# Matmuls of 96 and 128 output rows cut into column tiles of 32 rows, in a fused two-layer MetaFormer kernel

## The reference, cut to what matters

```python
# layer 0, conv block, MID = 576
h = silu(bn(einsum('nchw,oc->nohw', ln_c(x), w_exp)))          # 96 -> 576
h = silu(bn(depthwise_3x3(h, w_dw)))
s = sigmoid(silu(h.mean((2, 3)) @ w_se1.T + b_se1) @ w_se2.T + b_se2)
x = x + (bn(einsum('nchw,oc->nohw', h * s, w_proj)) + ln_c(x))  # 576 -> 96
# both layers, feed-forward, all operands rounded to fp8e5, sums to fp16
t = t + qlinear(relu(qlinear(ln_t(t), W1, b1)), W2, b2)         # 96 -> 384 -> 96
# layer 1, conv block
g = gelu(group_norm1(conv1x1(ln_c(x), w1, b1)))
g = gelu(w21 on two shifts of g) + gelu(w22 on two shifts of g) # four terms
x = x + conv1x1(group_norm1(g), w3, b3)
```

## Time and profile before

| | |
|---|---|
| median of 3 runs | 6858.68 us (6851.56 to 6858.77) |
| the profiled execution | 6854.27 us, its span 6852.4 us |
| PE busy | 5730.9 us, 84% of the span |
| DVE busy | 5543.4 us, 81% |
| ACT busy | 4409.0 us, 64% |
| mean granted TensorE clock | 0.959 |

### The profile page before, as it was taken

How to read it: one execution, slowest core, us unless ns; L and a number is a source line. 1 busy time by engine, 2 the same in 40 slices (tenths; PEclk the granted TensorE clock), 3 DMA queues, 4 the chain that set the end, 5 groups by cost and what they waited for, 6 DMA issues and landing times.

```text
span 6852.4 us, 111430 instructions
## 1 busy us (share of the span) xinstructions
PE 5730.9 (84%) x40192; PEld 2277.5 (33%) x40192; DVE 5543.4 (81%) x9325; ACT 4409.0 (64%) x7671; POOL 452.6 (7%) x366
## 2 busy tenths in 40 slices
PE   2788888888888888888888888888888888888875
PEld 0333333333333333333333333333333333333332
DVE  4788888888888888888888888888888888888863
ACT  1466766666766666766666766666766666766654
POOL 1000000000000000000000000000000000000000
PEclk9899999999999999999999999999999999999997
DMA  1233323333323333323323323333323323323322
GB/s 41 63 76 86 94 73 86 91 76 85 96 71 85 93 76 85 96 71 87 92 76 85 96 73 86 90 76 84 96 70 85 94 76 84 96 67 88 87 59 62
DMA packets 395481, 556.45 MB, mean 81 GB/s; under 512 B 71490, under 2 KB 391427, under 8 KB 391771
## 3 DMA queue, kind: packets, MB, share of 16 engines
q1 hardware_dynamic: 394940, 549.32, 31.7%
HBM read 233.66 MB, written 78.68 MB: 46 GB/s over the span
## 4 chain that ended last, share of the span: by engine, by line
PE 45%; DVE 31%; ACT 10%; DMA 6%; issue 5%; SPq 4%; DVEq 0%; ACTq 0%; POOL 0%; POOLq 0%
DVE conv L859 16%; PE bank L583 10%; PE bank L598 6%; PE bank L557 4%; PE bank L535 3%; PE bank L585 3%; PE b_banks L682 3%; PE b_banks L639 2%; PE bank L544 2%; DVE hidden L914 2%; PE b_banks L663 2%; ACT hidden L782 2%; PE b_banks L618 2%; DVE xn L906 2%; DVE x L924 2%
## 5 line engine op out<-in xcount | busy, mean ns | idle before, releaser
L859 DVE SCALAR_TENSOR_TENSOR conv<-mid,w_dw,conv 128x1568 f32<-128x1568 f32 x1536 | 2893.7, 1884 | 20.4
L663 PE MATMUL b_banks<-shifted,w_combo 128*32 128x392 f32 x6144 | 681.1, 580 | 311.9 <-DMA shifted<-g 257.8
L535 PE MATMUL bank<-xc_a,w_exp 128*128 128x392 f32 x1536 | 654.9, 525 | 110.1 <-DVE xc_a L842 34.0
L583 PE MATMUL bank<-conv,w_proj_gated 128*96 128x392 f32 x2048 | 728.8, 499 | 4.8 <-DVE x L885 0.5
L598 PE MATMUL bank<-x,centering 128*96 128x392 f32 x1536 | 645.1, 515 | 74.2 <-DVE x L924 39.5
L775 ACT ACTIVATE hidden<-b_banks 128x1176 f16<-128x1176 f32 x512 | 590.0, 1152 | 139.5 <-PE b_banks L618 135.0
L782 ACT ACTIVATE hidden<-hidden 128x1176 fp8e5<-128x1176 f16 x512 | 607.4, 1186 | 39.4 <-DVE hidden L914 39.2
L1001 POOL TENSOR_TENSOR x<-x,xc_a 96x392 f32<-96x392 f32 x256 | 433.2, 1693 | 1729.9 <-DVE xc_a L842 1729.9
L722 ACT ACTIVATE phases<-bank 128x448 f32<-128x448 f32 x384 | 208.5, 543 | 515.5 <-PE bank L544 422.6
L691 ACT ACTIVATE g<-bank 96x392 f32<-96x392 f32 x512 | 256.8, 502 | 337.9 <-PE bank L598 289.6
L618 PE MATMUL b_banks<-xn,w_q 128*128 128x392 fp8e5 x1536 | 348.4, 336 | 133.8 <-ACT hidden L775 116.8
(11 more groups left out here) (157 smaller groups left out, 8112.3 us busy)
## 6 DMA issues: line engine op xcount, KB each, us to landing
phases_on<-phases SPq DMA_DIRECT2D x768, 101.5 KB, 2.6
shifted<-g SPq DMA_DIRECT2D x512, 149.6 KB, 2.7
r_b<-rstd_row_b SPq DMA_DIRECT2D x512, 147.0 KB, 3.0
shifted<-g SPq DMA_DIRECT2D x256, 199.5 KB, 3.0
x<-in_x SPq DMA_DIRECT2D x32, 1176.0 KB, 8.0
r_a<-rstd_row_a SPq DMA_DIRECT2D x256, 147.0 KB, 3.2
x_plus_norm<-x SPq DMA_DIRECT2D x256, 147.0 KB, 2.8
r_a<-x_plus_norm SPq DMA_DIRECT2D x256, 147.0 KB, 2.5
```

Of the source, the lines that this page charges most:

```text
L535: mm(ring[bank][:, 0:TW], WEXP[:, 128 * k:128 * k + 128], xc_tile(t, 128), start=True, stop=True)\
L583: mm(o, WPS[:, k, :], tile(conv(k, t // NTH, parity), t % NTH, 128), start=(k == 0), stop=False)
L663: last = mm(rows(PB[32 * u:32 * u + 32, m, 0:TW]), WC[:, u // 2, 32 * m:32 * m + 32], SH[t % 2][:, u, :].rearrange("p (h w) -> p h w", w=G ...
L859: v.scalar_tensor_tensor(out=acc, in0=src, scalar=WDW[:, k, j:j + 1], in1=acc, op0=ALU.mult, op1=ALU.add).then_inc(sem["convolved"], 1)
```

## The change

A helper `columns` issues every product of 96 or 128 output rows as three or four matmuls of 32 output rows, each at its own output partitions, all with the same moving operand. All f32 full-width products and the fp8 products of `up` and `down` go through it; `se2`, the two `gn` steps and `gn_weights` stay as they were. The last chunk of `proj` now reads all 128 partitions of `ACC4`, with weights that are zero for the half that isn't the tile's; for this `WP` and `WPS` have a sixth chunk, the gate multiplies it in an instruction of its own, and the setup fills it.

```diff
+        def columns(o, weights, x, start=True, stop=True):
+
+            for j in range(0, weights.shape[-1], QUAD):
+                last = mm(o[j:j + QUAD, :], weights[:, j:j + QUAD], x, start=start, stop=stop)
+            return last
...
-                mm(ring[bank][:, 0:TW], WEXP[:, 128 * k:128 * k + 128], xc_tile(t, 128), start=True, stop=True)\
+                columns(ring[bank][:, 0:TW], WEXP[:, 128 * k:128 * k + 128], xc_tile(t, 128))\
                     .then_inc(sem["expanded"], 1)
...
                 for k in range(NCH):
-                    mm(o, WPS[:, k, :], tile(conv(k, t // NTH, parity), t % NTH, 128), start=(k == 0), stop=False)
-                h = t // NTH
-                mm(o, WPS[CW * h:CW * h + CW, NCH, :],
-                   ACC4[CW * h:CW * h + CW, (t % NTH) * TW:(t % NTH + 1) * TW], start=False, stop=True)\
+                    columns(o, WPS[:, k, :], tile(conv(k, t // NTH, parity), t % NTH, 128), start=(k == 0), stop=False)
+                columns(o, WPS[:, NCH + t // NTH, :], tile(ACC4, t % NTH, 128), start=False, stop=True)\
                     .then_inc(sem["projected"], 1)
...
                 for c in range(NHC):
-                    last = mm(PB[:, c, 0:TW], W1Q[:, f, 128 * c:128 * c + 128], XN8[t % 2][:, :],
-                              start=True, stop=True)
+                    last = columns(PB[:, c, 0:TW], W1Q[:, f, 128 * c:128 * c + 128], XN8[t % 2][:, :])
...
-                v.tensor_tensor(WPS[:, :, :], WP[:, :, :],
-                                GATE[:, 2, :].unsqueeze(2).to_broadcast([128, NCK, C]), ALU.mult)\
+                v.tensor_tensor(WPS[:, 0:NCK, :], WP[:, 0:NCK, :],
+                                GATE[:, 2, :].unsqueeze(2).to_broadcast([128, NCK, C]), ALU.mult)
+                v.tensor_scalar(WPS[CW:128, NCK, :], WP[CW:128, NCK, :], GATE[CW:128, 2, NCH:NCK], None, ALU.mult)\
                     .then_inc(sem["se_vector"], 1)
...
+        then(v.tensor_copy(WP[CW:128, NCK, :], WP[CW:128, NCH, :]))
+        then(v.memset(WP[CW:128, NCH, :], 0.0))
+        then(v.memset(WPS[:, :, :], 0.0))
```

More of the change, by code:

```diff
@@ L225, in program @@
     BSE2 = sb("b_se2", [128, NCK], fp32)
-    WP = sb("w_proj", [128, NCK, C], fp32)
-    WPS = sb("w_proj_gated", [128, NCK, C], fp32)
+    WP = sb("w_proj", [128, NCK + 1, C], fp32)
+    WPS = sb("w_proj_gated", [128, NCK + 1, C], fp32)
     SE1 = sb("w_se1", [128, NCK, SEH], fp32)
@@ L522, in tensor_steps @@
                 wait_bank(pe, prev)
-                mm(ring[bank][0:C, 0:TW], CEN[:, :], tile(XFULL[parity], t, 128), start=True, stop=True)\
+                columns(ring[bank][0:C, 0:TW], CEN[:, :], tile(XFULL[parity], t, 128))\
                     .then_inc(sem["centered_a"], 1)
@@ L597, in tensor_steps @@
                 wait_bank(pe, prev)
-                mm(ring[bank][0:C, 0:TW], CEN[:, :], tile(XFULL[1 - parity if L else parity], t, 128), start=True, stop=True)\
+                columns(ring[bank][0:C, 0:TW], CEN[:, :], tile(XFULL[1 - parity if L else parity], t, 128))\
                     .then_inc(sem["centered_b" if L else "centered_c"], 1)
@@ L626, in tensor_steps @@
                 for c in range(NHC):
-                    last = mm(ring[bank][0:C, 0:TW], W2Q[:, f, c, :], Q8[t % 2][:, c, :],
-                              start=(c == 0), stop=(c == NHC - 1))
+                    last = columns(ring[bank][0:C, 0:TW], W2Q[:, f, c, :], Q8[t % 2][:, c, :],
+                                   start=(c == 0), stop=(c == NHC - 1))
                 last.then_inc(sem["down_done"], 1)
@@ L638, in tensor_steps @@
                     pe.wait_ge(sem["conv1_evacuated"], at(NT * b + t - 2))
-                mm(PB[0:C, t % 3, 0:TW], WL1[:, 0, :], tile(GFULL, t, 128), start=True, stop=True)\
+                columns(PB[0:C, t % 3, 0:TW], WL1[:, 0, :], tile(GFULL, t, 128))\
                     .then_inc(sem["conv1_done"], 1)
@@ L681, in tensor_steps @@
                     pe.wait_ge(sem["conv3_added"], at(NT * b + t - 2))
-                mm(PB[0:C, t % 3, 0:TW], W3S[:, :], tile(GFULL, t, 128), start=True, stop=True)\
+                columns(PB[0:C, t % 3, 0:TW], W3S[:, :], tile(GFULL, t, 128))\
                     .then_inc(sem["conv3_done"], 1)
@@ L1013, in program @@
     loads = [(WEXP[0:C, :], w["w_exp"]), (bn1_rows, w["bn1"].partition_broadcast(C + 1)), (WT[:, :], w["w_phase"]), (BN[:, :, :], w["bn"]), (WDW[:, :, :], w["w_dw"]),
-             (BSE2[:, :], w["b_se2"]), (WP[:, :, :], w["w_proj"]), (SE1[:, :, :], w["w_se1"]),
+             (BSE2[:, :], w["b_se2"]), (WP[:, 0:NCK, :], w["w_proj"]), (SE1[:, :, :], w["w_se1"]),
              (SE2, w["w_se2"]), (BSE1, w["b_se1"]), (BN3[:, :], w["bn3"]),
```

2 lines of the change are left out of this document (1 added, 1 removed).

## The result

The changed kernel takes 6739.52 us (median of 4 runs, 6736.43 to 6742.2), the kernel before, run beside it, 6855.12 us (4 runs, 6844.88 to 6858.77). The ratio is 0.9834, 95% interval 0.9817 to 0.9851: 116 us, or 3.6 us per image, faster. The forecast was 168 us, 5.25 per image. One execution of the last kernel of the experiments ran at a granted clock of 0.562, where the others have 0.95 to 0.96, took 9569 us and is left out.

What follows compares the result with a forecast made beforehand. PE was taken to bound about 77 us of each 205.3 us period, DVE 128. Per image 4.6 + 1.3 - 0.25 - 0.4 = 5.25 us, x 32 = 168, giving 6691 us; range 6610 to 6815.

Steps and rivals of the forecast that it cites:

- What bounds the kernel: Of each 205.3 us period, about 77 us go by PE (3105 to 3182) and 128 by DVE.
- I take nothing: DVE stretches: 5.6 us of PE stops per period removed, no gain counted; up to 2 us kept for the upper case.
- The drain and the bare load: PE stops at changes of form, about 0.09 us; a first weight load hidden by nothing costs 0.08 to 0.11 us.
- The term of 4.6 us for the clean stretch: PE from 3129.55 to 3178.37, 48.8 us: 4.6 of 4.9 us of drains and bare loads go per image.
- Others take the place: PE stretch: DVE's order and fetched rows eat half or more of 5.9 us; about 2 us stay, 6795; 17%.
- The term of 1.3 us ahead of it: From 3109.9 up to the clean stretch: 1.3 of 2.7 us of drains and bare loads saved per image.
- The 0.25 us of the added DVE instruction: Ahead of `proj`, one 64x96 DVE instruction per image, taken as 0.25 us lost on the path.
- The 0.4 us of skew: Column tiles start some ns apart: 0.02 us lost for each of some 20 products on the path, per image.
- The fp8 columns run one after another: `up` and `down` tiles not side by side: 1.98 and 1.49 us instead of 0.49; 7105 us; 4%.
- The issue of matmuls sets the pace: fp8 sets need one matmul per 41 ns; at 82 ns, 2.75 us of the gain would stay, 6771; 5%.
- The stops stay: PE's stops come from something other than form; only added work is left, 21 us, 6880; 3%.
- The whole chain shortens: DVE stretches also give 2 us where PE and DVE are nearly tied: 8.8 us per image, 6575; 10%.

Runs made afterwards that it cites:

- the last kernel of the experiments: Last one listed: changed kernel with the gate's DVE entry and first `up` of layer b moved, `up` and `down` in full width; 6724.42 us, ratio 0.9818.
- two Newton steps: Third Newton step of every reciprocal root left out: in the kernel before 6825.11 us, ratio 0.9977; in the changed kernel 6645.59 us, ratio 0.9715.
- moving `up`: Changed kernel with the first `up` of layer b behind two `var` steps in PE's order: 6726.0 us, ratio 0.9817 to the kernel before.
- the gate's run: DVE's `se2` bias addition (L866) moved ahead of a `norm_a`: changed kernel 6719.7 us, ratio 0.9819; kernel before 6837.64 us, 0.9995.
- The four-column kernel: Changed kernel with a fourth column tile, repeating the first's weights and read by nobody, for each 96-row product: 6732.35 us, ratio 0.9842.

## Why the prediction was right, and what it sized wrong

- **What bounds the kernel.** Right for the PE stretches: 77 us of the period shown became 73.2. For the rest "I take nothing" was right in size for this change (by the table, 135.5 us behind the eighth addition became 135.2), but the reason given is only half of it. If DVE alone set the pace there, most of the 3.2 us that two Newton steps take from its work behind the clean stretch (three roots and one of the group norm) would have arrived in the kernel before; 0.5 us did. Stops and roots taken together gave 2.6. So PE and DVE are nearly tied there, and PE's slack "costs and gives nothing" only while the roots stay as long as they are.
- **The drain and the bare load.** Right in kind, and in size at each place that was named: these lost their stops. One form for the last chunk alone is worth 39 to 42 us.
- **The term of 4.6 us for the clean stretch.** It measured 2.4 as the mean of 25 periods (48.97 to 46.60 us) and 3.0 in the period shown (48.82 to 45.87), and this is where the forecast failed. The stops themselves were undersized: the 0.8 us of waits in the working held 0.7 that lie ahead of the stretch's first row, so 48.8 less 43.1 of passes left some 5.5 of stops, not 4.9. Of the 45.9 us after, 43.1 are passes, and nearly all of the other 2.8 are waits, 2.4 of them the five shown. So about 5 us of stops went, and 2 us of new waits came in this period and some 0.5 more in the mean one. The working said that "a wait for a fetched row that PE's lateness hides now will show", but only the rival *Others take the place* gave it a price; the sum had none. Its first row (0.46 us, with 0.16 more of pass end) could have been priced beforehand: `xn` in the kernel before was ready a fixed 9.1 us behind the third addition of `proj` (51.50 less 42.38 in the table, 9.24 after), and PE's work in those 9.1 us was counted to shrink. Shortening that root brought 0.7 us back and moving `up` the same, so this chain is shown as a part of the loss; the wait behind `x_plus_norm` (0.5 us on the mean) and those for ACT were seen and not taken away by any run.
- **The term of 1.3 us ahead of it.** It measured 0.65 to 0.7, and only 0.1 of it ahead of the first matmul of `proj` (14.91 us behind `se1` before, 14.81 after, over the 25 periods). There PE waits in turn for DVE, for ACT and for the group norm, and the gate's run shows one wait going over into the next.
- **The 0.25 us of the added DVE instruction.** It takes 0.27 us and lies off the path: `w_proj_gated` is done at 3063.44 and `proj` starts at 3067.36, behind the group norm. The term is nothing.
- **The 0.4 us of skew.** The four-column kernel puts it within the scatter, at most 0.3.
- **The sum.** 4.6 + 1.3 became 2.4 + 0.7, the two subtractions nearly nothing, and the rest of the period gave 0.3: 3.4 us per image by the table. That the sum came as near as it did is in part luck. The undersized stops (4.6 for some 5.5) and the 0.65 us subtracted for nothing both made up for waits that it left out; with these two put right it would have said 6.8 us, twice what came.
- **The signs.** Steps 0.66 us apart, `proj` in 3.3 us, fp8 steps of three passes and more idle time of PE came as said. The two waits of DVE for PE were to fall by about half and fell by 30%, and one sign of being wrong showed in part: DVE waits more for fetched rows, 148.7 us for 131.7 at `xn`.
- **The rivals.** *The fp8 columns run one after another*: no, 12 matmuls of `up` take 0.50 us, three passes. *The issue of matmuls sets the pace*: not at this rate, since 12 in 0.50 us are 41 ns each, and PE kept it. The Trainium skill (TensorE: Matmul & The Clock Gate, "Wait — 56ns, not 53.3ns?") gives about 62 ns per MATMUL where instructions aren't decoded in hardware. They don't appear here: by an estimate from that figure `up` would have been 0.74 us long. *The stops stay*: no. *Others take the place* was right as a mechanism with a part of its price, some 2.5 of the 5.9 us. *The whole chain shortens*: only with the roots shortened too.

## What to carry to other kernels

- Count how often the form of TensorE's products (full width, column tile, fewer partitions) changes along its sequence; each change cost a stop of about 0.1 us here, and the bare load behind it as much again. One form for all, even at more rows, is the gain, and the cheapest way (here one chunk on 128 partitions) may give a third of it. Converting a single product moves the stops to its borders (here `proj` alone gave 14 us, all of them together 116).
- Before pricing a faster engine, list the chains that run beside it in the same stretch with their fixed lengths (here 9.1 us through memory) and compare each with the new work of the engine: the gain ends where the first of them is longer.
- Look at many periods before taking a mean effect from one: here the period shown gained 3.0 us in the clean stretch and the mean one 2.4.
- A null result for one of two nearly equal chains says nothing of both. Shortening the root gave 16 us before the change and some 85 after it. Look again at such edits after each change that worked.

## What the runs showed of the hardware that I had not expected

A column tile that a 96-row product leaves free doesn't wait for the others: it starts the next step's matmul while the other three are still at this one. PE's timeline of the changed kernel:

```profile
3077.36 0.51 PE L510 MATMUL b_banks<-g,w_scaled 128*32 128x392 f32 x3
3077.38 0.52 PE L510 MATMUL bank<-xc_a,w_exp 128*32 128x392 f32 x1
3077.69 0.51 PE L510 MATMUL b_banks<-g,w_scaled 128*32 128x392 f32 x3
3077.73 1.12 PE L510 MATMUL bank<-xc_a,w_exp 128*32 128x392 f32 x7
```

The tile of `expand` that `conv3` leaves free, its last, runs 0.3 us ahead of its three fellows, beside the second pass of `conv3`. It stays one pass ahead and no more. Where the free tile has fp8 and its neighbours f32 (`up` inside `proj`, 3117.74 and 3118.07 in the same trace), its matmuls begin 0.33 us apart like the f32 passes beside them, not at the 0.17 us of fp8. What is read from the bank comes no earlier either: ACT's `mid` starts at 3078.93, 0.58 us behind the start of the other tiles' last pass. Running ahead gave no time that the four-column kernel, where no tile is free, would lack.
